# Half of the score columns of each context group as three products of high and low parts

## What is computed

```python
def _L0_xattn_ref(query, ref, Wq, bq, Wk, bk, Wv, bv):
    norm_fact = 1.0 / np.sqrt(HIDDEN).astype(np.float32)
    Q = query @ Wq + bq
    K = ref @ Wk + bk
    V = ref @ Wv + bv
    scores = jnp.einsum('bqh,bkh->bqk', Q, K)
    attn = jax.nn.softmax(scores, axis=-1) * norm_fact
    return jnp.einsum('bqk,bkh->bqh', attn, V)

x = x + _L0_xattn_ref(_layernorm(x, axis=-1), ctx_1024, ...)
x = x + _L0_attn_ref(_layernorm(x, axis=-1), ...)
x = x + _L0_ffn_ref(_layernorm(x, axis=-1), ...)
```

## Time and profile before

| | |
|---|---|
| time, median of 3 runs | 257.92 us (256.78 to 258.92) |
| profiled execution | 258.82 us, span of its instructions 257.0 us |
| mean granted TensorE clock | 0.985 |
| busy: PE, DVE, ACT, POOL | 238.8, 143.4, 131.9, 111.6 us |
| chain that ended last, shares | PE 74%, DVE 10%, issue 7%, POOL 3%, ACT 3% |

### The profile page before, as it was taken

How to read it: one execution, slowest core, us unless ns; L and a number is a source line. 1 busy time by engine, 2 the same in 40 slices (tenths; PEclk the granted TensorE clock), 3 DMA queues, 4 the chain that set the end, 5 groups by cost and what they waited for, 6 DMA issues and landing times.

```text
span 257.0 us, 4527 instructions
## 1 busy us (share of the span) xinstructions
PE 238.8 (93%) x1643; PEld 199.8 (78%) x1643; DVE 143.4 (56%) x324; ACT 131.9 (51%) x237; POOL 111.6 (43%) x59
## 2 busy tenths in 40 slices
PE   8899999999999997699959998999999999799985
PEld 6645777777777776599738997985579999699984
DVE  2116555555555553247892546345433898858982
ACT  5235555555555556268602052555334949439450
POOL 1066266666666666505799311000000647345450
PEclk9999999999999999999958999999999999999999
DMA  6999999999997969694000000000000048892000
GB/s 231 382 427 418 415 419 421 417 414 359 395 337 282 425 229 416 252 431 173 0 0 3 0 0 4 3 0 0 0 3 0 4 145 325 333 411 97 0 0 20
DMA packets 7233, 52.62 MB, mean 205 GB/s; under 512 B 809, under 2 KB 1074, under 8 KB 6194
## 3 DMA queue, kind: packets, MB, share of 16 engines
q1 hardware_dynamic: 7218, 52.43, 51.7%
HBM read 52.29 MB, written 0.13 MB: 204 GB/s over the span
## 4 chain that ended last, share of the span: by engine, by line
PE 74%; DVE 10%; issue 7%; POOL 3%; ACT 3%; DMA 1%; DVEq 1%; ACTq 0%; POOLq 0%
PE psum L373 35%; PE psum L424 12%; PE psum L368 8%; PE psum L661 5%; POOL ctx_lo L308 3%; PE psum L530 3%; PE psum L544 3%; DVE h_lo L1186 2%; DVE ring L1180 2%; PE psum L364 2%; PE psum L582 1%; PE psum L610 1%; DMA early_sb<-in_early 1%; PE psum L566 1%; PE psum L478 1%
## 5 line engine op out<-in xcount | busy, mean ns | idle before, releaser
L308 POOL TENSOR_TENSOR ctx_lo<-ring,ctx_hi 128x1792 fp32r<-128x1792 f32 x14 | 56.4, 4029 | 46.1 <-ACT ctx_hi L720 46.1
L373 PE MATMUL psum<-late_sb,work 128*128 128x448 f32 x112 | 46.4, 560 | 0.6 <-DVE work L919 0.6
L356 POOL TENSOR_TENSOR w_lo<-late_sb,w_hi 128x1280 fp32r<-128x1280 f32 x4 | 13.5, 3370 | 55.9 <-ACT w_hi L869 55.9
L373 PEld LDWEIGHTS psum<-late_sb,work 128*128 128x128 f32 x112 | 21.2, 199 | 17.8 <-issue 17.1
L727 ACT ACTIVATE probsT_hi<-psum 128x512 fp32r<-128x512 f32 (+1 forms) x28 | 13.7, 542 | 33.4 <-PE psum L368 33.4
L928 DVE TENSOR_REDUCE smalls<-psum 128x1 f32<-128x896 f32 x14 | 15.3, 1092 | 24.9 <-PE psum L373 24.9
L720 ACT ACTIVATE ctx_hi<-ring 128x1792 fp32r<-128x1792 f32 x14 | 23.8, 1700 | 6.6 <-DMA ring<-in_ctx 6.6
L373 PE MATMUL psum<-xT,late_sb 128*128 128x128 f32 x224 | 26.1, 276 | 0.1
L373 PEld LDWEIGHTS psum<-xT,late_sb 128*128 128x128 f32 x224 | 25.4, 192 | 0.3 <-DVE xT L1149 0.3
L424 PE MATMUL psum<-ctx_hi,probsT_hi 128*128 128x256 f32 x98 | 20.6, 326 | 2.9 <-POOL ctx_lo L308 1.8
L424 PEld LDWEIGHTS psum<-ctx_hi,probsT_hi 128*128 128x128 f32 x98 | 14.5, 191 | 7.8 <-issue 7.8
(11 more groups left out here) (220 smaller groups left out, 446.6 us busy)
## 6 DMA issues: line engine op xcount, KB each, us to landing
late_sb<-in_ctx_T SPq DMA_DIRECT2D x14, 896.0 KB, 9.9
ring<-in_ctx SPq DMA_DIRECT2D x14, 896.0 KB, 9.1
late_sb<-in_late SPq DMA_DIRECT2D x10, 825.0 KB, 10.1
late_sb<-in_experts SPq DMA_DIRECT2D x4, 2048.0 KB, 8.4
late_slots<-in_experts SPq DMA_DIRECT2D x4, 2048.0 KB, 7.7
early_sb<-in_early SPq DMA_DIRECT2D x1, 625.0 KB, 10.2
early_sb<-in_early SPq DMA_DIRECT2D x1, 512.0 KB, 3.7
early_sb<-in_early SPq DMA_DIRECT2D x1, 200.0 KB, 2.5
```

The lines of the kernel that those rows point to most:

```text
L308: nc.gpsimd.tensor_tensor(ctxNv[1][:, r % 2], ring[:, r], ctxNv[0][:, r % 2], ALU.subtract).then_inc(s["ctx_lo"], 1)
L356: nc.gpsimd.tensor_tensor(w2[1][:, j % 2, at], slot_w2(j)[:, at], w2[0][:, j % 2, at], ALU.subtract).then_inc(s["w2_lo_pool"], 1)
L373: last = nc.tensor.matmul(o, lhs(c), rhs(c), start=(c == 0), stop=(c == n - 1))
```

## The change

For each group from 2 on, the first half of the score columns is made from parts: T_hi and T_lo are the high and low parts of the transposed context (448 columns of each of the two channel chunks, 896 a group), G_hi and G_lo those of G. Six float32r products of 448 columns (three terms by two chunks) take the place of two plain float32 products. The other half stays plain and comes first. Groups 0 and 1 stay as they were.

ScalarE makes T_hi (`ctxT_hi_parts`), GpSimd T_lo (`ctxT_lo_parts`), into two buffers. ScalarE also makes G_hi and VectorE G_lo, once. TensorE waits for T_lo between the two halves. The new tensors lie in the memory into which the late2 transfers go, and so these move behind the wait for the last scores. ScalarE's and GpSimd's loops are now two rounds of four with the rest written out, in the same order.

```diff
         E_sb = sb("early_sb", EARLY_N)
+        with ExitStack() as overlay:
+            overlay.enter_context(nc.sbuf_tensor("first_parts", [P, FIRST_PARTS * PART_N], F32))
+            T_parts = [overlay.enter_context(nc.sbuf_tensor(f"ctxT_{part}", [P, 2 * DC * HALF], F32R)) for part in ("hi", "lo")]
+            G_parts = [overlay.enter_context(nc.sbuf_tensor(f"G_{part}", [P, D], F32R)) for part in ("hi", "lo")]
         W_sb = sb("late_sb", LATE_N + W_SLOTS * EXPERT_N)
...
+            sp.wait_ge(s["scores_ready"], NG)
             for i in range(FIRST_PARTS, LATE_PARTS):
                 part(i, "late2_in")
-            sp.wait_ge(s["scores_ready"], NG)
...
+            def ctxT_lo_parts(g, r):
+
+                pool.wait_ge(s["T_hi"], g - 1)
+                nc.gpsimd.tensor_tensor(Tv[1][:, r % 2], ringT[:, r, :, 0:HALF], Tv[0][:, r % 2], ALU.subtract).then_inc(s["T_lo"], 1)
+
+            ctx_lo_parts(0, 0)
+            ctxT_lo_parts(2, 2)
+            ctx_lo_parts(1, 1)
+            with pool.Fori(0, 2) as i:
                 for j in range(RING):
-                    ctx_lo_parts(i * RING + j, j)
...
+                    ctxT_lo_parts(i * RING + (j + 3), (j + 3) % RING)
+                    ctx_lo_parts(i * RING + (j + 2), (j + 2) % RING)
...
-                for hf in range(2):
+                for hf in ((0, 1) if first else (1,)):
                     last = wide(bank[2 * (r % 2) + hf][:, 0:HALF], lambda c: G[:, c * P:(c + 1) * P],
                                 lambda c: ringT[:, r, c, hf * HALF:(hf + 1) * HALF])
+                if not first:
+                    pe.wait_ge(s["T_lo"], g - 1)
+                    terms = [(a, b, c) for a, b in ((0, 0), (1, 0), (0, 1)) for c in range(DC)]
+                    for i, (a, b, c) in enumerate(terms):
+                        last = nc.tensor.matmul(bank[2 * (r % 2)][:, 0:HALF], half(G_parts[a], c), Tv[b][:, r % 2, c, :],
+                                                start=(i == 0), stop=(i == len(terms) - 1))
                 last.then_inc(s["scores_ready"], 1)
...
             probs_transposes(0, first=True)
+            pe.wait_ge(s["G_lo"], 1)
...
+            def ctxT_hi_parts(r, filled):
+
+                act.wait_ge(ctxT_in[r], filled)
+                nc.scalar.activation(Tv[0][:, r % 2], ringT[:, r, :, 0:HALF], ACT.Copy).then_inc(s["T_hi"], 1)
+
+            act.wait_ge(s["g_done"], 3)
+            nc.scalar.activation(G_parts[0][:, :], bank[6][:, 0:D], ACT.Copy).then_inc(s["G_hi"], 1)
             ctx_hi_parts(0, 0, 16, first=True)
+            ctxT_hi_parts(2, 16)
             ctx_hi_parts(1, 1, 16, first=True)
             exps(0, 0, first=True)
             probs_hi_parts(0, first=True)
-            with act.Fori(0, 3) as i:
+            with act.Fori(0, 2) as i:
                 for j in range(RING):
                     exps(i * RING + (j + 1), (j + 1) % RING)
                     probs_hi_parts(i * RING + (j + 1))
+                    ctxT_hi_parts((j + 3) % RING, i * 16 + (32 if j >= 1 else 16))
                     ctx_hi_parts(i * RING + (j + 2), (j + 2) % RING, i * 16 + (32 if j >= 2 else 16))
...
             dve.wait_ge(s["consts_set"], 4)
+            dve.wait_ge(s["G_hi"], 1)
+            V.tensor_tensor(G_parts[1][:, :], bank[6][:, 0:D], G_parts[0][:, :], ALU.subtract).then_inc(s["G_lo"], 1)
```

More of the change, by code:

```diff
@@ L143, in perceiver @@
         ctxNv = [part[:, :].rearrange("p (b t d) -> p b t d", b=2, d=D) for part in ctxN]
+        Tv = [part[:, :].rearrange("p (b c k) -> p b c k", b=2, c=DC) for part in T_parts]
         probsT = [part[:, :].rearrange("p (t q) -> p t q", q=T) for part in PT]
@@ L198, in perceiver @@
             ln_var ln_sd ln_xn ln_T ln_xT q_ready q_done g_ready g_done bv_ready
-            ctx_hi ctx_lo probsT_hi scores_ready max_ready exp_done alpha_done probs_transposed probsT_lo pv_done acc_done
+            G_hi G_lo T_hi T_lo ctx_hi ctx_lo probsT_hi scores_ready max_ready exp_done alpha_done probs_transposed probsT_lo pv_done acc_done
             o_T o_copied att_ready
@@ L308, in ctx_lo_parts @@
                 nc.gpsimd.tensor_tensor(ctxNv[1][:, r % 2], ring[:, r], ctxNv[0][:, r % 2], ALU.subtract).then_inc(s["ctx_lo"], 1)
-            with pool.Fori(0, 3) as i:
-                for j in range(RING):
-                    ctx_lo_parts(i * RING + j, j)
-            for g in range(3 * RING, NG):
-                ctx_lo_parts(g, g % RING)
+            def ctxT_lo_parts(g, r):
[5 more added lines that the diff above has]
+            with pool.Fori(0, 2) as i:
+                for j in range(RING):
+                    ctxT_lo_parts(i * RING + (j + 3), (j + 3) % RING)
+                    ctx_lo_parts(i * RING + (j + 2), (j + 2) % RING)
+            for g in range(2 * RING, NG - 2):
+                if g + 3 < NG:
+                    ctxT_lo_parts(g + 3, (g + 3) % RING)
+                ctx_lo_parts(g + 2, (g + 2) % RING)
             pool.wait_ge(s["pv_done"], NG)
@@ L737, in _ @@
                     probs_hi_parts(i * RING + (j + 1))
+                    ctxT_hi_parts((j + 3) % RING, i * 16 + (32 if j >= 1 else 16))
                     ctx_hi_parts(i * RING + (j + 2), (j + 2) % RING, i * 16 + (32 if j >= 2 else 16))
+            for g in range(2 * RING, NG - 2):
+                exps(g + 1, (g + 1) % RING)
+                probs_hi_parts(g + 1)
+                if g + 3 < NG:
+                    ctxT_hi_parts((g + 3) % RING, 16 * ((g + 3) // RING + 1))
+                ctx_hi_parts(g + 2, (g + 2) % RING, 16 * ((g + 2) // RING + 1))
             exps(NG - 1, (NG - 1) % RING)
```

## The result

The changed kernel takes 301.39 us (median of 4 runs, 299.09 to 303.27) against 258.42 us for the kernel before: a ratio of 1.170, 95% interval 1.164 to 1.176. It is slower, as forecast, but the time lies outside the range of 278 to 292 us. The profiled execution has a span of 301.5 us, with a mean granted clock of 0.914 (0.985 before); it is the slowest of the four, and the spans of the others are 297.3 to 299.7 us at 0.924 to 0.935.

The account below looks back on a forecast made before the run. TensorE was taken to bound the group loop, at 6.29 us a period. Profiled 258.82 us + 2.05 (start) + 23.3 (eleven waits) = 284.2, or 283.3 by the median; forecast 283.7 us, range 278 to 292.

Parts of the forecast that it names:

- Direction and mechanism: Group loop: slower (0.96), as T_hi queues behind probs_hi and only the plain half, 1.5 us, covers the split.
- The sizes of the wait: Group loop: T_hi 0.93 us, T_lo 2.09, period from 6.29 to 8.41 us; 11 x 2.12 = 23.3 us.
- rival (b): Part products in the scores: 448 columns cost as much as a float32 record, 0.376 us; 297 us; 3%.
- the clock: Group loop: sum taken at full clock, granted clock 1.00 throughout, though a rule on the clock suggested more loss.
- two rows of before: Earlier profile: clock stayed 1.00 over 102 to 106 us, but was 0.50 after 125 to 131 us.
- nearer the second: New loop's idle time, s + 1.5 to s + 3.9 in 8.4 us, placed nearer the case with clock 0.50.
- Rival (a): Group loop: clock falls in the waits, every second period low at 12.8 us, mean growth 4.3; 308 us; 8%.
- The start: Before the loop: T_hi(2), awaiting its transfer until 20.0, delays exps(0); 2.05 us late, low 1.2, high 3.
- The tail: Behind the loop: the last ctx_lo holds attend(13) by the same steps, so the length stays unchanged.
- Transfers, semaphores and volumes at nothing: Late2 transfers slip some 25 us harmlessly, added TensorE semaphores find events past, GpSimd's 6.13 us of 8.41 no bound.

Follow-up runs that it names:

- e4: Changed kernel with ScalarE making T_hi(g+3) ahead of probs_hi(g+1) instead of behind it; 264.12 us, ratio 1.026 to the kernel before.
- e3: Changed kernel with the parts made but unused: both score halves plain, no TensorE wait for T_lo; 261.32 us, ratio 1.013 to the kernel before.
- e2: Changed kernel with 10 filler products on TensorE between the plain half and the wait for T_lo; 289.88 us, ratio 1.127 to the kernel before.
- e5: Changed kernel with 5 filler products on TensorE between the plain half and the wait for T_lo; 287.99 us, ratio 1.116 to the kernel before.
- e6: Changed kernel with T_hi ahead of probs_hi, ctx_hi(0) before G_hi, T_hi(2) behind exps(0), T_lo on VectorE before probs_lo; 256.74 us, ratio 0.997.
- e7: Kernel before with parts made one group further ahead, four buffers, T_lo on VectorE behind probs_lo, split from group 6 on; 255.29 us, ratio 0.991.
- e8: Changed kernel with only ScalarE's start reordered: ctx_hi(0) before G_hi, T_hi(2) behind exps(0); 298.16 us, ratio 1.157 to the kernel before.

## Why the prediction was wrong

**Direction and mechanism: right.** T_hi stands behind probs_hi, which waits for the transposes, and so the split of a group starts when its scores do. e4 shows it by moving that one call; e3, without the wait and the part products, runs at the old period.

**The sizes of the wait: right.** T_hi 0.95 us (0.93 said), T_lo 2.08 (2.09), part products at s + 3.89 (3.92), a period at full clock of 8.47 to 8.50 us (8.41). The products of 448 columns cost 0.203 us each (in e2 the six take from 64.20 to 65.51, 1.31 us, of which 0.09 are the refilling), a little over the 0.19 I took; rival (b) is out. Eleven waits cost 24.2 us, 23.3 said.

**The step that failed: the clock.** I put the new loop between two rows of before, called it "nearer the second", and summed at full clock, with nothing for the clock. Rival (a), with 8%, is what came. The runs showed 9 of 11 periods with a stretch at 1.2 GHz, 13.9 us in the loop and 2.8 behind it. I judged by how busy single windows were. The harmless waits of before, 1.2 and 1.8 us, were shorter and came once each, while here 2.2 us come in every period; which of the two matters more, no run tells apart. With 2.2 us of idle time in every period the clock fell nearly every time, with 1.1 us (e5) in none of the eleven. The length of a single wait isn't all of it: the same two waits stand behind the loop after the change (1.24 and 1.78 us), and there the clock did go to 0.50, at 147.2, which it did not before or in e2. The Trainium skill (TensorE: Matmul & The Clock Gate, section on how oscillation of the clock gate bites in real kernels) describes a loop of this kind, in which a wait in every tile, drawn there as some 3 to 5 us, brought the clock to half each time. The trace agrees in kind, with shorter waits, 2.2 us, and 9 periods of 11.

**Rival (a) itself was priced too high, at 308.** I took a whole period at half clock, every second time. In the trace it is some 3.4 us of nearly every period, 1.55 us lost each.

**The start: 3.6 us, 2.05 said.** The order of events was right, with T_hi(2) held up by its transfer until 19.03 (20.0 said) and ahead of exps(0). But TensorE stood idle for 4.66 us before transposes(0), and these and most of scores(2) ran at half clock (0.50 from 22.6 to 26.5). In e4, whose start is the same code, the clock read 1.00 there and the loop began at 30.20, 1.9 us late, about what was said. Other starts of the same steps are not alike either: scores(0) began at 9.97 here and at 12.90 before. Before, the products of G had started later (9.59 instead of 7.89) and taken 2.08 us instead of 1.16, and scores(0) itself ran at half rate, as I had read from the earlier trace rows; why one start is slow and another isn't, no run shows. The granted clock reads 1.00 over that stretch all the same (12.90 to 21.24 in the earlier trace rows), so there the column contradicts the distances of the records.

**The tail: 2.8 us, none said.** The granted clock was 0.50 from 147.2 to 154.0. With the wait filled the tail is 159.9 us, 0.4 from before; so it was the clock here as well.

**Transfers, semaphores and volumes at nothing: right.** In e3 all conversions run in the old period. Nothing waited for late2.

The final sum, by what was measured: 257.0 + 3.6 + 24.2 + 13.9 + 2.8 = 301.5.

## What to carry to other kernels

Where work is split off to other engines for an operand, find the instruction that stands ahead of it in each queue and ask what that one waits for; here moving one call gave back 37 of the 43 us. A wait that returns in every period of a TensorE-bound loop may have to be counted twice, once for its length and once for the clock: here 2.2 us a period did, 1.1 us did not. A few filler products tell the two apart in one run. And before VectorE is given a subtraction of two SBUF tensors beside GpSimd's, see whether the two would run at the same moment.

## What the runs showed of the hardware

- The clock can fall behind the idle time. In the windows shown above it went to 0.50 some 1.2 us after the wait's end, in the middle of full work: the records next to the wait look healthy and the slow ones stand behind them. In others it fell within 0.2 us of the wait's end, as in this one, where two part products take 0.75 us start to start instead of 0.41 (kernel after, timeline):

```profile
112.88 0.98 PE L425 MATMUL psum<-ctxT_hi,G_hi 128*128 128x448 f32 x2 [2.29 <-POOL ctxT_lo L318]
...
113.66 0.95 PE L425 MATMUL psum<-ctxT_hi,G_lo 128*128 128x448 f32 x2
...
114.41 0.95 PE L425 MATMUL psum<-ctxT_lo,G_hi 128*128 128x448 f32 x2
```

- VectorE's subtraction of two SBUF tensors does not run beside GpSimd's. In e6 eleven of twelve were issued under ctx_lo, from 0.6 to 2.0 us ahead of its end. They took 1.52 to 2.95 us and all ended 0.94 to 0.96 us after ctx_lo's end, so next to nothing of them ran beside it. The twelfth, and all eight of e7, in GpSimd's idle time but for the last 0.1 us, took 1.08 us. GpSimd's own time stayed at 4.05 us. VectorE's probsT_lo, with one input from PSUM, takes 0.68 to 0.69 us for 512 columns in e5, e6, e7 and e8 alike. The Trainium skill says so (SBUF — State Buffer, section Who interferes with whom, and the one on the two separate sides): the pair of ports that VectorE and GpSimd share is held for a whole instruction, and only instructions with two SBUF inputs or a 2-port mode need it on VectorE's side. The traces agree, with these numbers.
